# Gate weights as the stationary operand in four column groups, its logits turned by one transpose, and the query and key projections in rounds 6, 8, 9 and 12

## The reference

```python
def attention(x):                       # x: layernorm of the input, [16, 512, 256]
    q, k, v = x @ Wq + bq, x @ Wk + bk, x @ Wv + bv        # 16 heads of 16
    scores = where(|i - j| <= half, q k^T / 4, -1e30)
    out = softmax(scores) v, then W_o per head
    return out @ Wfc + bfc
def experts(X):                         # X: layernorm of x + attention
    gating = softmax(X @ Wg + bg)       # Wg: [256, 8]
    top2 = two largest gates and their experts
    return (sum of gate * expert(X) over top2) @ Wf + bf
x = x + attention(layernorm(x)); x = x + experts(layernorm(x))
```

## Time and profile before

| | |
|---|---|
| median of 3 runs | 1512.9 us (1511.43 to 1518.19) |
| the profiled execution | 1508.1 us, of which the span from first to last instruction is 1506.3 us |
| granted TensorE clock over the span | 0.898 of full speed |
| PE / DVE / ACT / POOL busy | 84% / 64% / 53% / 43% of the span |
| setup | up to about 110 us |
| attention part | about 110 to 950 us |
| expert part | from about 950 us |

### The profile page before, as it was taken

How to read it: one execution, slowest core, us unless ns; L and a number is a source line. 1 busy time by engine, 2 the same in 40 slices (tenths; PEclk the granted TensorE clock), 3 DMA queues, 4 the chain that set the end, 5 groups by cost and what they waited for, 6 DMA issues and landing times. The chain is left out here.

```text
span 1506.3 us, 46512 instructions
## 1 busy us (share of the span) xinstructions
PE 1270.5 (84%) x18200; PEld 930.1 (62%) x18200; DVE 968.7 (64%) x2064; ACT 798.4 (53%) x1388; POOL 647.7 (43%) x682
## 2 busy tenths in 40 slices
PE   6667888888788878887887773699999999999996
PEld 5534455554445545544555442588888888888885
DVE  4224668777776686778756656366666666666664
ACT  1344756666456655664554530355555555555554
POOL 2031422535345435354543645254455545544445
PEclk9867998998888888989987765799999999999999
DMA  6455464654545545545463232446654475464543
GB/s 130 166 130 145 99 188 102 174 128 127 161 127 142 149 105 173 132 122 162 113 171 98 88 99 85 106 66 122 126 113 66 66 175 69 64 123 67 66 64 48
DMA packets 226026, 175.35 MB, mean 116 GB/s; under 512 B 129082, under 2 KB 193082, under 8 KB 225866
## 3 DMA queue, kind: packets, MB, share of 16 engines
q1 hardware_dynamic: 167050, 116.62, 31.5%
q0 software_dynamic: 25728, 33.78, 13.0%
q10 hardware_dynamic: 33088, 22.71, 5.7%
HBM read 66.32 MB, written 89.40 MB: 103 GB/s over the span
## 5 line engine op out<-in xcount | busy, mean ns | idle before, releaser
L977 DVE TENSOR_REDUCE mx<-p_max 128x4 f32<-128x736 f32 (+1 forms) x256 | 219.1, 856 | 183.5 <-PE p_max L1248 179.2
L811 ACT ACTIVATE probs<-p_exp,unscale 128x736 f32<-128x736 f32 (+1 forms) x256 | 210.1, 821 | 206.3 <-PE p_exp L1248 204.4
L1491 PE MATMUL p_h<-xt_parts,w_hi 128*128 128x256 f16 x1824 | 273.7, 273 | 1.9 <-DVE xt_parts L1579 1.9
L1583 DVE SCALAR_TENSOR_TENSOR t<-p_h,b,t 128x256 f32<-128x256 f32 x272 | 131.0, 484 | 159.0 <-ACT t L1530 155.0
L1628 POOL DMA_INDIRECT out<-yw,tokens x136 | 211.9, 1558 | 28.3 <-POOL tick L1627 18.4
L1530 ACT ACTIVATE t<-p_h,b,undo 128x256 f32<-128x256 f32 x272 | 149.0, 559 | 91.8 <-PE p_h L1491 86.1
L1627 POOL TENSOR_TENSOR tick<-tick 128x1 f32<-128x1 f32 x136 | 82.9, 610 | 265.5 <-ACT yw L1547 265.5
L1491 PEld LDWEIGHTS p_h<-xt_parts,w_hi 128*128 128x128 f16 x1824 | 178.3, 98 | 22.7 <-DVE t L1583 2.1
L1491 PE MATMUL p_h<-xt_parts,w_lo 128*128 128x256 f16 x912 | 174.0, 273 | 0.0
L1241 PE MATMUL p_max<-mask,ident_bf 64*64 64x368 bf16 (+1 forms) x1024 | 93.8, 356 | 89.3 <-DVE mx L977 87.7
L706 POOL DMA_INDIRECT routed<-rows,slots x128 | 128.9, 1007 | 47.7 <-issue 47.7
(11 more groups left out here) (240 smaller groups left out, 2697.9 us busy)
## 6 DMA issues: line engine op xcount, KB each, us to landing
qk_dram<-qk_hi SPq DMA_DIRECT2D x128, 128.0 KB, 2.6
qs<-qk_dram SPq DMA_DIRECT2D x64, 192.0 KB, 4.2
ks<-qk_dram SPq DMA_DIRECT2D x64, 192.0 KB, 4.7
x_in<-in_x SPq DMA_DIRECT2D x64, 128.0 KB, 3.2
qk_dram<-qk_lo SPq DMA_DIRECT2D x64, 128.0 KB, 2.7
w_mat<-in_W ACTq DMA_DIRECT2D x32, 256.0 KB, 4.4
out<-x_sb SPq DMA_DIRECT2D x64, 128.0 KB
w_split<-w_first_hi SPq DMA_DIRECT2D x24, 256.0 KB
```

What stands on the lines that cost most here:

```text
L811: nc.scalar.activation(probs[r % 3][:, :, 0:hi - lo].rearrange("p (e s) w -> p e s w", e=2), p_exp[:, :, 0:2 * WIN].rearrange("p e (s w) - ...
L977: nc.vector.tensor_reduce(out=maxes, in_=p_max[:, :, 0:2 * WIN].rearrange("p e (s w) -> p e s w", s=2)[:, :, :, 0:hi - lo], axis=AX.X, op= ...
L1491: last = nc.tensor.matmul(p_h[:, m % KC, k, :], w[e][a][:, k, HID * c + P * m:HID * c + P * m + P], xt[:, x, c, :], start=(n == 0 and c == ...
L1583: nc.vector.scalar_tensor_tensor(t3[m // 2][:, m % 2, :], p_h[:, m % KC, 1, :], kept["b13"][:, 1, e, m:m + 1], t1[m][:], ALU.add, ALU.mult ...
```

## The change

The gate's weights become the stationary operand. `keep["wg"]` is widened from 8 to 32 columns, the added ones are zero (DVE clears the tile, and the load of `Wg` waits for that). `gate_logits` runs in round 14 as before, with one product for each token tile and depth half, each in its own group of 32 columns of the array (`tile_position=(0, 32 t)`), and 128 moving columns. The logits then lie in `p_sh` with experts on the partitions, so ACT copies them out (`logit_rows`, 128x128, round 14), and PE turns them with one transpose (`turn_logits`, round 15). DVE's `logits` reads that, in round 0 of the next step instead of round 15.

The four projections of a batch run in rounds 6, 8, 9 and 12 instead of 6, 9, 12 and 15, and ACT's copies with them. On POOL the fourth difference moves from the head of the next step to just behind the third. A step has 16 jobs instead of 15.

```diff
-             7: ("R", -2, 0), 9: ("QK", 3, 1), 10: ("G", -1, 0), 11: ("G", -1, 1), 12: ("QK", 3, 2), 13: ("M", 1, 0),
-             14: ("G", -1, 2), 15: ("QK", 3, 3)}
+             7: ("R", -2, 0), 8: ("QK", 3, 1), 9: ("QK", 3, 2), 10: ("G", -1, 0), 11: ("G", -1, 1), 12: ("QK", 3, 3), 13: ("M", 1, 0),
+             14: ("G", -1, 2), 15: ("G", -1, 3)}
+QK_SLOTS = (6, 8, 9, 12)
+GW = 32
...
+            def logit_rows(b):
+                bank, _, full = job("G", b, 2)
+                act.wait_ge(s_full[bank], full)
+                nc.scalar.activation(lg_rows[:], p_sh[:, bank, 0:P], ACT.Copy).then_inc(s_free[bank], 1)
...
-                bank, _, full = job("G", b, 2)
+                bank, _, full = job("G", b, 3)
                 dve.wait_ge(s_full[bank], full)
-                nc.vector.scalar_tensor_tensor(lg[:], p_sh[:, bank, 0:NT * NE].rearrange("p (t e) -> p t e", t=NT), 1.0 / X_SCALE,
+                nc.vector.scalar_tensor_tensor(lg[:], p_sh[:, bank, 0:P].rearrange("p (t e) -> p t e", t=NT)[:, :, 0:NE], 1.0 / X_SCALE,
...
-            for t in range(NT):
-                for c in range(NC):
-                    last = nc.tensor.matmul(p_sh[:, bank, 8 * t:8 * t + 8], xt2[:, c, P * t:P * t + P], keep["wg"][:, c, :],
-                                            start=(c == 0), stop=(c == NC - 1))
+            for c in range(NC):
+                for t in range(NT):
+                    last = nc.tensor.matmul(p_sh[GW * t:GW * t + GW, bank, 0:P], keep["wg"][:, c, :], xt2[:, c, P * t:P * t + P],
+                                            start=(c == 0), stop=(c == NC - 1), tile_position=(0, GW * t), skip_group_check=True)
...
+            def turn_logits(b):
+                bank = shared("G", b, 3)
+                taken(pe, s_free, "G", b, 2)
+                nc.tensor.transpose(p_sh[:, bank, 0:P], lg_rows[:], keep["ident"][:]).then_inc(s_full[bank], 1)
```

More of the change, by code:

```diff
@@ L735, in _ @@
             for i in STEPS:
-                if exists(i + 2) and i > FIRST_STEP:
-                    split_qk(i + 2, 3)
                 if exists(i - 2):
@@ L899, in _ @@
                             high_rows(i - 1)
+                        if n == 14:
+                            logit_rows(i - 1)
                     if loaded_expert(i) is not None:
@@ L1147, in _ @@
                     if exists(i - 2):
+                        if n == 0:
+                            logits(i - 2)
                         if n == 2:
@@ L1172, in _ @@
                             residual_out(i - 1)
-                        if n == 15:
-                            logits(i - 1)
                     if exists(i - 2) and n == 8:
@@ L1355, in _ @@
                             gate_logits(i - 1)
+                        if n == 15:
+                            turn_logits(i - 1)
                     if exists(i - 2) and n == 7:
```

16 lines of the change are left out of this document (10 added, 6 removed).

## The result

The changed kernel takes **1502.6 us** (median of 20 runs, 1494.92 to 1510.3) against 1511.49 us for the kernel before beside it (20 runs): a ratio of **0.9948**, 95% interval 0.9931 to 0.9965. It is 8.9 us faster. The forecast was 19.6 us faster; the sign was right, the size less than half. The profiled execution of the changed kernel has a span of 1498.0 us at a granted clock of 0.902, against 1506.3 us before.

What follows compares the result with a forecast made beforehand. In most rounds DVE waits for PE's scores, so PE's other work sets the pace. Terms -17.0 - 5.5 + 0.5 + 2.4 = -19.6 us take the 1512.9 us median to 1493.3 us, range 1481 to 1509.

Steps and rivals of the forecast that it cites:

- The gate and the turn: PE, rounds 14 and 15: gate 0.6 us instead of 1.95, added transpose 0.3; with the projection moved, 2.4 us shed.
- The four groups: Gate on PE: its column groups overlap; the rival that they don't (0.04) keeps it near 1.95 us, total 1504 us.
- Odd to even: Six step boundaries without weights to split, where PE is late: gates' division ends earlier, -17.0 us in all.
- POOL's limit of 11.85 us: Odd to even boundaries: POOL's low parts end 11.8 us after DVE's statistics, so the gates' division ends at 11.85.
- Even to odd: Four boundaries where POOL works without a gap: gates' division still ends 18.1 us after the statistics, gain 0.
- the more than 3.3 forecast: Sign at even to odd boundaries: the gates' division, held by POOL, takes more than 3.3 us of its own.
- The 1.0 us: Round 0: PE's scores for the exponentials start 1.0 us earlier, of 2.4 shed; lost waiting for POOL at even to odd.
- The other boundaries: Boundaries 0 to 1, 2 to 3, 12 to 13, 13 to 14: 1.0 us each, -4.0; with the end of step 15, -5.5.
- Rounds 8 and 9: Moved projections fill PE's idle time, +0.5 us; POOL's second difference holds DVE's product in steps 4, 6, 11, +2.4.
- The half clock: Rival, 0.18: PE idles longer and one more product or projection per step runs at half clock, 17 us, total 1510.
- The hold by POOL: Rival, 0.10: DVE's division escapes POOL's hold at the four even to odd boundaries, 17 us more gain, total 1476.
- ACT didn't take PE's place: Rival, 0.06: ACT's copies in rounds 8 and 9 delay exponentials and round 10's copy, +32 us, total 1525.

Runs made afterwards that it cites:

- e13: Changed kernel with two maxima transfers, repeated PE transposes in round 3 of four steps, and 7/8 of POOL's low parts omitted (not first expert): 1477.2 us, 0.9802 of the kernel before.
- e3: Changed kernel without the row of negated maxima in the exponentials' scores and without PE's wait for its transfers (computes something else): 1496.4 us, 0.9897 of the kernel before.
- e12: Changed kernel with DVE's logits read in round 15 again instead of round 0, third chip: 1496.6 us, 0.9928 of the kernel before.
- e9: The changed kernel run again unaltered on a third chip: 1502.6 us, 0.9971 of the kernel before.
- e16: Changed kernel with two maxima transfers, logits in round 15, and needless PE transposes in rounds 3 (four steps) and 10: 1477.5 us, 0.9795 of the kernel before.
- e18: Changed kernel with two maxima transfers and needless PE transposes in rounds 3 (four steps) and 10, logits in round 0: 1482.1 us, 0.9816 of the kernel before.
- e1: Changed kernel with projections back in rounds 6, 9, 12, 15 and POOL's fourth difference back at the next step's start: 1506.2 us, 0.9963 of the kernel before.
- e5: Changed kernel with DVE's logits read in round 15 again, on the second chip: 1565.4 us, 1.0045 of the kernel before.
- e7: Changed kernel with two maxima transfers and repeated PE transposes in round 3 of steps 5, 7, 9, 11, second chip: 1566.0 us, 1.0063 of the kernel before.
- e8: The kernel before with the maxima brought by two transfers instead of four, second chip: 1555.2 us, 0.9970 of the unaltered kernel before.

## Why the prediction was wrong, step by step

- **The gate and the turn** were right: 0.57 and 0.27 us against 0.6 and 0.3, ACT's copy 0.27. Rounds 14 and 15 together are 2.5 us shorter (7.19 to 4.67 us between DVE's maxima, means of steps 2 to 13), forecast 2.4. The four groups do overlap.
- **Odd to even, -17.0**: measured -10.7. This is the step that failed first and most, by 6.3 us. POOL's limit of 11.85 us was right within 0.05 us where it was reached (steps 1, 3 and 5: 11.80, 11.87 and 11.85), but in steps 7, 9 and 11 the gates ended 14.0, 14.2 and 15.2 us after the statistics. I asked who is late next among POOL, DVE and ACT, and left SP out: its transfers of the maxima, complete by the estimate above 0.4 us before PE needed them, are the next limit, and behind the long waits for them the values of round 0 run at half clock. With two transfers the same boundaries give -19.0.
- **Even to odd, 0**: the number was right, and in part by luck. In steps 4, 6, 8 and 10 the division ended 18.08 or 18.09 us after the statistics, with POOL's run, and e13 shows that POOL was the limit. But its row is 1.7 to 2.9 us, not the more than 3.3 forecast, because the division started 0.25 to 1.6 us later after the statistics than before, not earlier. The 1.0 us is there at first: in 8 to 9 `p_exp` of round 0 starts 7.06 us after the statistics, before 7.94. Then it is lost. PE had stood idle for 1.59 us, where the fourth projection had filled the time before, and it works through the values at half clock. The changed kernel, `p_exp`, the first values and the next maxima's scores:

```profile
563.92 0.42 PE L1252 MATMUL p_exp<-mask,ident_bf 64*64 64x248 bf16 x4 [1.59 <-ACT probs L815]
...
565.27 0.42 PE L1240 MATMUL p_sh<-wv_hi,xh 128*64 128x128 f16 x4
...
567.98 0.52 PE L1252 MATMUL p_max<-mask,ident_bf 64*64 64x368 bf16 x4
```

  The kernel before, values and scores of the same round:

```profile
573.09 0.30 PE L1229 MATMUL p_sh<-wv_hi,xh 128*64 128x128 f16 x4
...
574.55 0.35 PE L1241 MATMUL p_max<-mask,ident_bf 64*64 64x368 bf16 x4
```

  The values take 2.71 us instead of 1.46. In steps 1 to 13 of the kernel before they take 1.46 everywhere; in the changed kernel they take 2.2 to 2.7 us in ten of the thirteen, 10.5 us more in all. At these four boundaries POOL hides it.
- **The other boundaries, -4.0 of the -5.5**: measured +1.5, so this step failed too. Here too the 1.0 us that "counts" is lost again in the half clock, and nothing hides it: 2 to 3 grew by 2.8 us, with the same 1.59 us of idle time and 2.7 us of values in round 0 (the logits are held there for 1.16 us, but before it was 1.59). In e3 these values take 1.46 us, and the boundary grew by 0.1. At 12 to 13, which grew by 2.3 us, the logits in round 0 are held for 8.36 us. I had checked the new place at one boundary, 8 to 9, where DVE comes to it 7 us after the statistics while POOL scatters; at 12 to 13 there is no batch 16 whose statistics POOL would wait for, and its run of weight parts starts right with DVE's subtraction. In e12 that boundary is 1.0 us shorter than before. All that the shift of the logits costs comes to 6 us by e12 against e9.
- **Rounds 8 and 9, +2.9**: round 8 was right (no change: 2.57 us against 2.60, means of steps 3 to 12). Round 9 grew by 2.3 us in steps 3 to 12 together, where 2.4 was forecast, but that is luck. The steps in which POOL's second difference had missed DVE's product are 5, 7 and 12; the 4, 6 and 11 of the prediction are their batches. It falls beside the product there now, and round 9 grew by 1.2, 0.8 and 2.5 us; in the seven other steps it became 2.2 us shorter in all, from 1.3 us less to 0.1 more, for which nothing was put down.
- **Round 12, nothing put down**: this failed too. It grew by 0.4 us (2.01 to 2.42, steps 2 to 13), 6.8 us over steps 0 to 13 and so more than the whole row "inside" of the table. PE comes late to the projection there, out of rounds 10 and 11 at half clock. The transposes of round 10 ran at half clock before too, in many steps; those of round 11 did so in five of the steps 2 to 13, now in eleven. In step 9 of the changed kernel:

```profile
597.44 1.08 PE L1215 MATMUL p_sh<-ident,x2n 128*128 128x128 f32 x4 [2.55 <-DVE x2n L941]
...
600.62 1.11 PE L1215 MATMUL p_sh<-ident,x2n 128*128 128x128 f32 x4
```

  The second row before (the first is in the earlier trace rows):

```profile
610.00 0.65 PE L1204 MATMUL p_sh<-ident,x2n 128*128 128x128 f32 x4
```

  With that wait filled the transposes take 0.66 us there in e16 and e18, and round 12 is 1.33 us in steps 5, 7, 9 and 11 instead of 1.7 to 2.8.
- **The rivals.** The half clock (0.18; 1510 us) came true in part, though not in the product that it was read from: the output products are on the whole no slower than before (3.78 us in steps 5 and 7, 1.99 in 9 and 11), but the values of round 0 and the transposes of round 11 are, and both lie behind rounds that shed or moved a projection. The hold by POOL didn't give way (18.1 us). ACT didn't take PE's place in rounds 8 to 10: the sign named for it, no idle time before ACT's copy of round 10, isn't there (2.54 us of it in step 9, 1.4 us or more in steps 2 to 15). The other true rival, a transfer that becomes the limit, stood in no case. The range of 1481 to 1509 held the time. By the table the forecast gain was short in three places, not in one: 6.3 us odd to even, 5.5 at the other boundaries, 3.0 inside the steps.

The Trainium skill (DMA: Bandwidth & Descriptors, Anatomy of one DMA) gives a transfer a fixed cost of about 2.0 us whatever its size, fitted on GpSimd's path; the 2.6 to 2.7 us from SP's last issue to PE into steps 10 and 12 are of that order, for 4 KB each, the 1.2 us into the other even steps are well below it. With 0.3 us for ACT's copy and 2.47 to issue, that figure would have given an estimate of 4.8 us from the copy to PE; measured are 4.2 to 5.7.

## What to carry to other kernels

Before work is taken off the engine that sets the pace, list everything that its next instructions wait for, the small transfers of another queue too, and write beside each by how much it is early: the smallest slack caps the gain. An elementwise instruction with two inputs in SBUF that is moved needs its new place checked against POOL at every kind of boundary, not at one. A long product that stands between a wait and short products may also be what keeps the clock up, so taking it out can cost what it gives: compare the rows behind it. Where PE idles for some microseconds ahead of long products, repeating a harmless product there can be worth more than the edit itself; whether the rows behind it really get faster has to be looked up, since in the kernel before they didn't.

## What the hardware did that I had not expected

- **POOL's hold runs across its instructions.** L1041 in e1 began 0.44 us ahead of POOL's first weight part, beside the last scatter, and ended only after five of POOL's instructions, 9.92 us. In the changed kernel the same subtraction at 563.75 us, beside a scatter, took 0.19. The Trainium skill (SBUF — State Buffer, Who interferes with whom) says that a DVE instruction with two inputs in SBUF contends with a GpSimd instruction that reads SBUF, and that the order of issue decides who blocks. Here DVE's is ahead of the first weight part in the record, and it waits through all of them. What decides between the two cases I can't say.
- **PE can stand with nothing to wait for.** On the second chip the kernels e5 to e7 have 44 to 52 us of gaps of over 0.25 us in PE's rows marked "issue" (the profile shows nothing that PE waited for), e8 32 us, where the kernels on the other chips have 0 to 2.4. The cause isn't shown. In the values of round 0 of e5:

```profile
645.05 0.32 PE L1240 MATMUL p_sh<-wv_lo,xh 128*64 128x128 f16 x4 [0.28 <-issue]
645.82 0.22 PE L1240 MATMUL p_sh<-wv_hi,xl 128*64 128x128 f16 x1 [0.45 <-issue]
646.51 0.30 PE L1240 MATMUL p_sh<-wv_hi,xl 128*64 128x128 f16 x3 [0.48 <-issue]
```

  All three variants of the changed kernel were slower than the kernel before there (1.0045 to 1.0063). The bare changed kernel didn't run on that chip, so whether its gain holds there is open.
